# Gated experts with an FFN: the FFN weight's quantisation taken from the end of the job sequence into its middle, and the last expert's squares from GpSimd to ScalarE

## The reference

```
x = x + tanh(g_xattn) * experts(layernorm(x))
    # experts: for each token's expert e, W = ctx[e]
    #   a = h W^T;  z = silu(a) * a;  y = z W^T
x = x + tanh(g_ffn) * ffn(layernorm(x), weight)
    # ffn: w_scale = max|weight| / 448;  w8 = e4m3(weight / w_scale)
    #      x_scale = max|x| / 448;       x8 = e4m3(x / x_scale)
    #      bf16((x8 @ w8^T) * x_scale * w_scale)
```

## Time and profile before

| What | Value |
|---|---|
| three executions, median | 211.3 us (209.51 to 211.76) |
| profiled execution | 211.72 us, span in the trace 210.0 us |
| mean granted clock of TensorE | 0.919 of full speed |
| busy in the span | PE 153.3, DVE 160.4, ACT 112.5, POOL 89.7, PEld 75.5 us |

### The profile page before, as it was taken

How to read it: one execution, slowest core, us unless ns; L and a number is a source line. 1 busy time by engine, 2 the same in 40 slices (tenths; PEclk the granted TensorE clock), 3 DMA queues, 4 the chain that set the end, 5 groups by cost and what they waited for, 6 DMA issues and landing times.

```text
span 210.0 us, 3410 instructions
## 1 busy us (share of the span) xinstructions
PE 153.3 (73%) x759; PEld 75.5 (36%) x764; DVE 160.4 (76%) x348; ACT 112.5 (54%) x167; POOL 89.7 (43%) x120
## 2 busy tenths in 40 slices
PE   0233859299999999999999999999631559386800
PEld 0102324134455555545554554554210234232300
DVE  2896797897947687788788759879985996987810
ACT  2465694258554576576557653563215967545600
POOL 6168788703303434432343433126420033564870
PEclk9999978969999999999999999999996587959985
DMA  3838997000000000000000000000000011222341
GB/s 47 334 111 219 405 376 199 15 0 2 0 3 0 2 0 0 0 0 0 0 0 0 0 3 0 0 3 0 2 0 0 0 50 50 100 102 101 150 173 76
DMA packets 5642, 13.24 MB, mean 63 GB/s; under 512 B 1024, under 2 KB 1536, under 8 KB 5632
## 3 DMA queue, kind: packets, MB, share of 16 engines
q0 software_dynamic: 2560, 8.39, 11.2%
q1 hardware_dynamic: 2784, 4.73, 6.5%
q10 hardware_dynamic: 288, 0.00, 0.1%
HBM read 8.92 MB, written 4.19 MB: 62 GB/s over the span
## 4 chain that ended last, share of the span: by engine, by line
PE 50%; DVE 22%; issue 10%; POOL 8%; ACT 5%; DMA 1%; DVEq 1%; POOLq 0%; ACTq 0%
PE four_ps L442 12%; PE four_ps L450 12%; PE four_ps L455 11%; PE four_ps L559 4%; PE four_ps L482 4%; POOL out L342 4%; PE four_ps L433 3%; DVE w_bits L758 3%; POOL x L319 3%; DVE w_hi L1029 2%; PE four_ps L446 2%; DVE hT_hi L1037 2%; ACT w_hi L586 2%; DVE x L1041 2%; ACT y L684 1%
## 5 line engine op out<-in xcount | busy, mean ns | idle before, releaser
L342 POOL DMA_INDIRECT out<-x,token_of x16 | 20.5, 1283 | 27.7 <-DVE x L1041 24.6
L350 POOL TENSOR_TENSOR z<-az,sg 128x512 f32<-128x512 f32 x15 | 19.1, 1271 | 30.5 <-ACT az L610 21.5
L337 POOL TENSOR_TENSOR rstd<-var,minus_half 128x1 f32<-128x1 f32 x16 | 11.1, 692 | 45.3 <-DVE var L869 45.3
L608 ACT ACTIVATE sg<-four_ps,job_inv_a 128x512 f32<-128x512 f32 x19 | 13.0, 686 | 25.5 <-PE four_ps L455 19.9
L442 PE MATMUL four_ps<-w_hi,hT_hi 128*128 x76 | 21.8, 401 | 4.5 <-ACT w_hi L586 4.2
L442 PE MATMUL four_ps<-w_hi,zT_hi 128*128 x76 | 19.5, 379 | 1.4 <-DVE x L855 1.4
L319 POOL DMA_INDIRECT x<-in_x,token_of x16 | 17.4, 1089 | 7.0 <-issue 4.2
L559 PE MATMUL four_ps<-wf_q,qT 128*128 128x512 bf16 x61 | 19.9, 474 | 0.3 <-issue 0.2
L450 PE MATMUL four_ps<-w_lo,hT_hi 128*128 x76 | 20.0, 386 | 0.0
L617 ACT ACTIVATE zT_hi<-four_ps 128x512 f16<-128x512 f32 x19 | 11.3, 594 | 16.3 <-PE four_ps L482 16.3
L855 DVE SCALAR_TENSOR_TENSOR x<-four_ps,job_mul,x 128x512 f32 x19 | 14.2, 748 | 7.2 <-PE four_ps L455 7.1
(11 more groups left out here) (150 smaller groups left out, 303.4 us busy)
## 6 DMA issues: line engine op xcount, KB each, us to landing
w<-in_ctx_t SPq DMA_DIRECT2D x4, 1024.0 KB, 9.0
wf<-in_wf_t SPq DMA_DIRECT2D x1, 512.0 KB, 14.6
x<-in_x,token_of POOLq DMA_INDIRECT x16, 5.7
out<-x,token_of POOLq DMA_INDIRECT x16, 3.2
g_s<-in_g_x ACTq DMA_DIRECT2D x1, 0.5 KB, 2.8
ids_s<-in_ids SPq DMA_DIRECT2D x1, 8.0 KB, 2.5
g_s<-in_g_f ACTq DMA_DIRECT2D x1, 0.5 KB, 6.5
```

Of the source, the lines that this page charges most:

```text
L342: pool.indirect_dma_start(out, bass.IndirectOffsetOnAxis(ap=token_of[:, i:i + 1], axis=0), block_of(x1, i), None, bounds_check=T - 1).then ...
L350: pool.tensor_tensor(z[:, :], az[:, :], sg[:, :], ALU.mult).then_inc(z_done, 1)
```

## The change

1. POOL no longer squares the last expert's matrix. ACT does it, four instructions at the end of its job 1, behind the first normalisation of tile 3.
2. The loops on POOL, ACT and DVE are written out in full; PE's loop starts at job 8 in place of job 4.
3. The quantisation of the weight moves. DVE takes the maximum in halves at the end of its jobs 5 and 6, joins them and fills `diag` after job 6; PE spreads it after its job 7; DVE computes scale and inverse after job 7; ACT computes |w|/scale and w/scale for one quarter at the end of each of its jobs 8 to 11; DVE computes the grid of one quarter at the end of jobs 9 to 12, from |w|/scale directly and without the bit mask; POOL does both rounding steps of one quarter at the end of jobs 10 to 13. DVE does no rounding any more. Nothing of it is left in jobs 14 to 18.

The diff, in the order of the file: POOL, PE, ACT, DVE.

```diff
+        WF_MAX, WF_ONES, WF_SCALED, WF_GRID, WF_ROUNDED = 5, 7, 8, 9, 10
...
-                if isinstance(j, int) and JOBS - 2 <= j < JOBS:
...
                 if not isinstance(j, int) or E <= j:
                     rstd_second(j - E)
+                if WF_ROUNDED <= j < WF_ROUNDED + K:
+                    wf_rounded(j - WF_ROUNDED)
+
+            def wf_rounded(k):
+                cols = wf_part(k)
+                pool.wait_ge(wfm_done, k + 1)
+                pool.tensor_tensor(wf_v[:, cols], wf_v[:, cols], wf_m[:, cols], ALU.add).then_inc(wft_done, 1)
+                pool.wait_ge(wft_done, k + 1)
+                pool.tensor_tensor(wf_q[:, cols], wf_v[:, cols], wf_m[:, cols], ALU.subtract).then_inc(wfq_done, 1)
...
-            last_square(0)
-            job(1)
-            for k in range(1, K):
-                last_square(k)
...
+            for j in range(1, TILES + E):
                 job(j)
...
-            for j in range(E):
+            for j in range(WF_ONES + 1):
                 job(j)
+            pe.wait_ge(pool_const, 12)
+            pe.wait_ge(wf_step, 4)
+            pe.matmul(m_ps[:, 0:P], ones_f[:, :], diag[:, :], start=True, stop=True).then_inc(wf_max_done, 1)
+            with pe.Fori(WF_ONES + 1, TILES - 2, 2) as j:
...
-            pe.wait_ge(wfq_done, K // 2)
-            pe.wait_ge(wfs_done, 1 + K // 2)
+            pe.wait_ge(wfq_done, K)
...
+                if fixed and j == 1:
+                    squares(3)
+                if fixed and WF_SCALED <= j < WF_SCALED + K:
+                    wf_scaling(j - WF_SCALED)
+
+            def wf_scaling(k):
+                cols = wf_part(k)
+                act.wait_ge(wf_scaled, 1)
+                act.activation(wf_a[:, cols], wf[:, cols], ACT.Abs, scale=wf_inv[:, :]).then_inc(wfa_done, 1)
+                act.activation(wf_v[:, cols], wf[:, cols], ACT.Copy, scale=wf_inv[:, :]).then_inc(wfv_done, 1)
...
-                if j == TILES:
-                    act.wait_ge(wf_scaled, 1)
-                    act.activation(wf_v[:, :], wf[:, :], ACT.Copy, scale=wf_inv[:, :]).then_inc(wfv_done, 1)
...
+            def wf_half(n):
+                dve.wait_ge(wf_loaded, 16)
+                dve.tensor_reduce(wf_max[:, n:n + 1], wf[:, n * 2 * D:(n + 1) * 2 * D], AX.X, ALU.max,
+                                  apply_absolute_value=True).then_inc(wf_step, 1)
+
+            def wf_spread():
+                dve.wait_ge(wf_step, 2)
+                dve.tensor_tensor(wf_max[:, 2:3], wf_max[:, 0:1], wf_max[:, 1:2], ALU.max).then_inc(wf_step, 1)
+                dve.wait_ge(wf_step, 3)
+                dve.tensor_scalar(diag[:, :], ident[:, :], wf_max[:, 2:3], None, ALU.mult).then_inc(wf_step, 1)
...
+            def wf_grid(k):
+                cols = wf_part(k)
+                dve.wait_ge(wfa_done, k + 1)
+                dve.wait_ge(wfv_done, k + 1)
+                dve.tensor_scalar(wf_m[:, cols], wf_a[:, cols], 1.5 * 2.0 ** -6, 2.0 ** 20, ALU.max, ALU.mult)\
+                    .then_inc(wfm_done, 1)
...
+            for j in range(TILES + E + 1):
                 job(j)
+                if WF_MAX <= j < WF_MAX + 2:
+                    wf_half(j - WF_MAX)
+                if j == WF_MAX + 1:
+                    wf_spread()
+                if j == WF_ONES:
+                    wf_scaling()
+                if WF_GRID <= j < WF_GRID + K:
+                    wf_grid(j - WF_GRID)
```

More of the change, by code:

```diff
@@ L121, in gated_experts_kernel @@
         diag = sb("diag", [P, P], F32)
-        wf_max = sb("wf_max", [P, 2], F32)
+        wf_max = sb("wf_max", [P, 4], F32)
         wf_scale = sb("wf_scale", [P, 1], F32)
@@ L157, in gated_experts_kernel @@
         wf_v = sb("wf_v", [P, K * D], F32)
-        wf_e = sb("wf_e", [P, K * D], BF16)
+        wf_a = sb("wf_a", [P, K * D], BF16)
         wf_m = sb("wf_m", [P, K * D], BF16)
@@ L243, in w_block, with wf_part @@
             return t[:, bass.ds(e * (K * D) + k * D, D)]
+        WF_MAX, WF_ONES, WF_SCALED, WF_GRID, WF_ROUNDED = 5, 7, 8, 9, 10
+        def wf_part(k):
+            return slice(k * D, (k + 1) * D)
         def tiles_of(g):
@@ L376, in _ @@
                     rstd_first(after_gather[i])
-            def last_square(k):
-                pool.wait_ge(w_loaded[E - 1], 16)
-                pool.tensor_tensor(w_block(w_lo, E - 1, k).bitcast(BF16), w_block(w32, E - 1, k),
-                                   w_block(w32, E - 1, k), ALU.mult).then_inc(last_squares, 1)
-            last_square(0)
-            job(1)
-            for k in range(1, K):
-                last_square(k)
-            for j in range(2, E + 1):
-                job(j)
-            with pool.Fori(E + 1, TILES - 2) as j:
-                job(j)
-            for j in range(TILES - 2, TILES + E):
+            for j in range(1, TILES + E):
                 job(j)
@@ L525, in _ @@
                 job(j)
-                if j == TILES - 1:
-                    pe.wait_ge(pool_const, 12)
-                    pe.wait_ge(wf_step, 2)
-                    pe.matmul(m_ps[:, 0:P], ones_f[:, :], diag[:, :], start=True, stop=True).then_inc(wf_max_done, 1)
             down(JOBS - 1, expert_of(JOBS - 1))
@@ L653, in _ @@
             w_high(1)
-            for j in range(E + 1):
+            for j in range(TILES + E + 1):
                 job(j)
@@ L657, in _ @@
                     act.wait_ge(w_lo_done, K * E)
-            with act.Fori(E + 1, TILES - 2) as j:
-                job(j)
-            for j in range(TILES - 2, TILES + E + 1):
-                job(j)
-                if j == TILES:
-                    act.wait_ge(wf_scaled, 1)
-                    act.activation(wf_v[:, :], wf[:, :], ACT.Copy, scale=wf_inv[:, :]).then_inc(wfv_done, 1)
             def scaled(g):
@@ L924, in job @@
                     max_second(j - E - 2)
-                if fixed and j == JOBS - 1:
-                    for k in range(K // 2, K - 1):
-                        wf_rounded(k)
                 if not fixed or j + 1 < TILES:
@@ L966, in _ @@
             w_low(1, [1, 2])
-            for j in range(E + 2):
+            for j in range(TILES + E + 1):
                 job(j)
-            for i in range(E + 4, TILES):
-                dve.wait_ge(x_gathered[i], 16)
-            with dve.Fori(E + 2, TILES - 2) as j:
-                job(j)
-            for j in range(TILES - 2, TILES + E + 1):
-                job(j)
-                if j == TILES - 2:
-                    dve.wait_ge(wf_loaded, 16)
-                    dve.tensor_reduce(wf_max[:, 0:1], wf[:, :], AX.X, ALU.max, apply_absolute_value=True)\
-                        .then_inc(wf_step, 1)
-                    dve.wait_ge(wf_step, 1)
-                    dve.tensor_scalar(diag[:, :], ident[:, :], wf_max[:, 0:1], None, ALU.mult).then_inc(wf_step, 1)
-                if j == TILES - 1:
-                    dve.wait_ge(wf_max_done, 1)
-                    routed(dve.tensor_reduce(wf_max[:, 1:2], m_ps[:, 0:P], AX.X, ALU.max))
-                    routed(dve.tensor_scalar(wf_scale[:, :], wf_max[:, 1:2], 1.0 / E4M3_MAX, 1e-12, ALU.mult, ALU.max))
-                    dve.reciprocal(wf_inv[:, :], wf_scale[:, :]).then_inc(wf_scaled, 1)
-                if j == TILES:
-                    dve.wait_ge(wfv_done, 1)
-                    dve.tensor_scalar(wf_e[:, :].bitcast(I16), wf_v[:, :].bitcast(I16)[:, 1::2], EXP_MASK >> 16, None,
-                                      ALU.bitwise_and).then_inc(wfe_done, 1)
-                    dve.wait_ge(wfe_done, 1)
-                    dve.tensor_scalar(wf_m[:, :], wf_e[:, :], 2.0 ** -6, 1.5 * 2.0 ** 20, ALU.max, ALU.mult)\
-                        .then_inc(wfm_done, 1)
-                if j == JOBS - 2:
-                    cols = slice(K // 2 * D, K * D)
-                    dve.wait_ge(wfm_done, 1)
-                    dve.tensor_tensor(wf_v[:, cols], wf_v[:, cols], wf_m[:, cols], ALU.add).then_inc(wfs_done, 1)
-                if j == JOBS - 1:
-                    wf_rounded(K - 1)
+                if WF_MAX <= j < WF_MAX + 2:
[6 more added lines that the diff above has]
+                    wf_grid(j - WF_GRID)
             dve.wait_ge(nmr2_done, TILES)
```

25 lines of the change are left out of this document (7 added, 18 removed).

## The result

| | before | after |
|---|---|---|
| median of four executions | 211.3 us (209.51 to 211.76) | 204.15 us (204.08 to 204.28) |
| profiled execution, span | 211.72, 210.0 us | 204.08, 202.2 us |
| mean granted clock | 0.919 | 0.947 |

The changed kernel is faster: ratio 0.971, 95% interval 0.9654 to 0.9765.

The account below looks back on a forecast made before the run. In steady jobs PE's work and the chain silu, az, z were both taken to fill the 6.1 us. The terms -3.8 - 2.1 + 3.6 + 4.6 = +2.3 gave a median of 213.6 us, range 209.3 to 217.0.

Parts of the forecast that it names:

- part 3: Jobs 5 to 9: maximum, spreading and scaled weight make h, silu and z late; 3.6 us slower, bounds 1.5 and 5.5.
- part 4: Jobs 10 to 13: POOL's rounding delays z, 1.4 us first, then 1.1 each; 4.6 us slower, bounds 3.6 and 5.6.
- part 1: First jobs: without POOL's squares w_bits gets through when z ends, at 37.2; gain 3.8 us, bounds 3.0 and 4.5.
- part 2: Last jobs: the quantisation work that leaves them shortens PE's waits; gain 2.1 us, bounds 1.4 and 3.0.
- chain of delays: Jobs 5 to 9: h late by 0.6 to 0.7, then 0.9, then 0 to 0.6, then ACT's first pair.
- unrolled loops cost nothing I can see: Loops on ACT, DVE and POOL: engines wait where branches stood; between 0.4 us gained and 0.4 us lost.
- its race with z: Job 6: nmr loses to POOL's z by about 0.1 us; if nmr won, jobs 5 to 9 would cost 3.0, not 3.6.
- The tail itself is unchanged: After the last jobs: the tail keeps its length, with no gain or loss counted for it.
- The rival on the clock: Steady jobs: PE's gaps lower its clock; one job at 1.2 GHz costs 5.2 us, giving 218.8; chance 0.06.
- the port: A DVE instruction with two SBUF inputs waits beside POOL instructions that read SBUF; w_bits took 4.57 us against 0.72.
- The pause on DVE is absorbed: Rival, jobs 5 to 9: nmr and the join get ahead of z, cost only 1.0 to 1.5, time 211.2; chance 0.18.
- The faster front: Rival: first jobs gain 4.5, last jobs 3.0, pause costs 1.2, rounding repeats 0.75 each; -2.7 us, 208.6; chance 0.12.

Follow-up runs that it names:

- max_whole: The changed kernel with the weight's maximum as one DVE instruction after job 5 in place of two halves; 204.64 us.
- unroll_only: The kernel before with its loops on POOL, ACT and DVE written out and PE's loop from job 8, nothing else; 210.49 us, ratio 0.9974.
- scaled_later: The changed kernel with ACT's pairs, DVE's grids and POOL's rounding steps one job later; 204.82 us.
- round_between: The changed kernel with POOL's two rounding steps between rstd1 and rstd2 in place of behind rstd2; 203.44 us, ratio 0.967 to the kernel before.
- late_tail: The changed kernel with one unused DVE maximum ahead of the last one, so that the tail starts 1.1 us later; 207.08 us.
- fill_before: The kernel before with unused matmuls put into PE's idle time in the tail; 208.32 us, ratio 0.9874.
- bits_one_input: The kernel before, squares still on POOL, with w_bits computed by four DVE instructions of one SBUF input each; 208.31 us, ratio 0.9864.

## Why the prediction was wrong

By its own parts, predicted against measured:

| part | predicted | measured |
|---|---|---|
| 1, squares | -3.8 | -5.2 |
| 2, last jobs | -2.1 | -2.3 |
| 3, jobs 5 to 9 | +3.6 | +0.5 |
| 4, rounding | +4.6 | +2.6 |
| tail, "unchanged" | 0 | -3.4 |
| sum | +2.3 | -7.8 |

Of the 10.1 us between +2.3 and -7.8 the tail is 3.4, part 3 is 3.1, part 4 is 2.0, part 1 is 1.4 and part 2 is 0.2. Two steps failed, a chain of delays in part 3 and the tail that was put at nothing; parts 4 and 1 had mis-sized terms.

**Part 3 is the step whose mechanism failed.** The chain of delays began with "h starts about 0.3 behind it and ends at 79.8: PE is 0.6 to 0.7 late", and each later term stood on that. From the end of z (76.1) to the end of h (79.8) the prediction has 3.7 us, built from distances in the loop: 1.85 from nmr to the end of hT_lo, then the addition, then 0.3 to h. Written out, the same path takes 3.05: in max_whole, and in job 7 of the changed kernel (z ends at 76.84, h at 79.90). The 0.6 between them is the predicted delay. Off the path the written-out code gives DVE 0.6 us a job (unroll_only), of which the prediction had given back the 0.44 of the branch and no more; its "unrolled loops cost nothing I can see" looked only at the path. The nmr of job 6 did win its race with z, by 0.06 us, and max_whole shows that it need not have. The measured +0.5 is against 30.53 in the loop; it is 0.7 against unroll_only's 30.27: 0.22 for the spreading matmul, which I had priced rightly, and 0.5 for ACT's first pair behind a late h, which I had priced at 0.5 to 1.3 (scaled_later shows the 0.5).

**Part 4** had the right mechanism, its terms mis-sized: the first delay of PE is 7.06 - 6.05 = 1.0 (95.89 to 102.95), predicted 1.4; the repeats are 6.66 - 6.05 = 0.6 each, predicted 1.1. rstd2 follows z by 3.8 us (101.63 to 105.42) in place of 4.5, so 0.7 less and not "some 0.35 less". Against the loop's 6.1 the sum is 2.6. round_between shows that place and not amount was what cost.

**Part 1** had the right mechanism and a term too small. I held the end of w_bits at 37.2, with z at 35.91; z started at 34.85, and w_bits ended at 36.15. What I had missed is that the first of POOL's squares stood ahead of z in POOL's list (it ended at 35.97) and leaves too. late_tail tells this from the clock, since its trace has the early half-speed stretch (29.3 to 32.7) that before had (29.4 to 32.8) and the changed kernel had not:

```profile
35.11 1.26 POOL L354 TENSOR_TENSOR z<-az,sg 128x512 f32<-128x512 f32 x1 [0.27 <-issue]
...
36.11 0.28 DVE L746 SCALAR_TENSOR_TENSOR w_bits<-scale_coef,half_f,scale_off 128x4 int32<-128x4 f32 x1
```

There z starts 0.8 us earlier than before, w_bits ends at 36.39 and job 3 is at 53.03. So of the 5.2 us, 4.3 are w_bits (40.72 to 36.39), 0.2 is the early stretch of the clock, and 0.6 lies behind w_bits, where the clock of before was at half from 43.0 to 46.4. The reading that w_bits stood "until POOL's row of reading instructions had a gap" is open: in the changed kernel it got through as z ended, though rstd1 followed as closely there (36.07) as it had before (37.13).

**The tail** was the assumption that I didn't price ("The tail itself is unchanged"), and it is the largest single miss. I had the troughs of the clock in the earlier trace rows and read them as given. They were worth 3.8 us in the profiled execution (fill_before). The tail of the changed kernel fell on a better place, by luck as far as the runs show: late_tail has the same instructions 1.1 us later and 48.2 us. The rival on the clock looked only for new slow stretches in the steady jobs, where none came (PEclk 9 throughout), and not for old ones that might go. Its argument that a gap of 1.39 us alone doesn't slow PE is not borne out: in fill_before the same gap, ahead of 150.40, is followed by half clock from 150.8.

What held: the place and sign of parts 1, 2 and 4, and the port in the earlier trace rows. Part 2 held by its terms too: jobs 16 and 17 take 11.2 us, and the last transpose of z to the next matmul 1.37 in place of 2.05. Of the signs, the w_bits of 1.09 us and the z that starts as a rounding step ends came; transposes of z 6.8, 8 and 7.3 apart in jobs 7 to 9 did not (6.05, 6.28, 6.50).

Two rivals were nearer than the forecast. *The pause on DVE is absorbed* (0.18) had the mechanism of part 3: nmr ahead of z in job 6 (69.46 and 69.52), the join ahead of z in job 7 (74.91 and 75.57); it priced part 3 at 1.0 to 1.5 and the time at 211.2. *The faster front* (0.12) came true by its own condition, repeats under 0.8, and without the tail's 3.4 us the profiled execution still gained 4.4, where this rival had 2.7. Neither had a term for the tail. The bounds of the four parts, added up as they stand, go from 208.9 to 218.0, not from 211.4 to 216.0, and 204.15 lies outside them as well.

The Trainium skill, "SBUF — State Buffer", section "Who interferes with whom", said of DVE instructions with two SBUF inputs what bits_one_input then measured: 0.34 us with one input, 3.90 for w_lo with two, beside the same row of POOL instructions. On the clock, "TensorE: Matmul & The Clock Gate", Part 1, says that the hardware's look at the engine's activity is free-running and isn't reset when a kernel starts. That agrees with executions of one program that differ by up to 3.0 us (the kernel before in the first group, 208.67 to 211.71) and with late_tail; no run here shows the cause itself.
